# First attention: each iteration's value products split in two column groups, with the maxima's products between them

## The reference, cut to what matters

```python
# x: 2 batches x 1024 tokens x 128; 16 heads, 8 numbers a head for q and k, 64 for v
cp = leaky_relu(einsum('btd,cd->btc', representations, Wc) + bc)
q, k, v = ...                                    # (2, 1024, 16, 8), (2, 1024, 16, 8), (2, 1024, 16, 64)
scores = einsum('bqhd,bkhd->bhqk', q, k) / 8 ** 0.5
attn = softmax(scores, axis=-1)
out = einsum('bhqk,bkhd->bqhd', attn, v).reshape(2, 1024, 1024)
proj = leaky_relu(einsum('btv,dv->btd', out, Wo) + bo)
```

## Time and profile before

| | us |
|---|---|
| median of 3 runs | 991.14 (988.55 to 994.42) |
| the profiled execution's own time | 985.0 |
| its span | 983.2 |
| first attention in that span (from 152 to 608) | 456 |

### The profile page before, as it was taken

How to read it: one execution, slowest core, us unless ns; L and a number is a source line. 1 busy time by engine, 2 the same in 40 slices (tenths; PEclk the granted TensorE clock), 3 DMA queues, 4 the chain that set the end, 5 groups by cost and what they waited for, 6 DMA issues and landing times. The chain is left out here.

```text
span 983.2 us, 20738 instructions
## 1 busy us (share of the span) xinstructions
PE 894.0 (91%) x7627; PEld 471.3 (48%) x7627; DVE 766.7 (78%) x1324; ACT 537.4 (55%) x903; POOL 599.2 (61%) x533
## 2 busy tenths in 40 slices
PE   4899997999999999899998999789999778799996
PEld 2356562233333333233332233679887444478695
DVE  6997789888888888998888852894589999983413
ACT  2154455666766676566666676454365334375463
POOL 3670327668887776878698876106527787572323
PEclk9899998999999999999999999999999999999999
DMA  9362364011111201102111113548761001253562
GB/s 314 117 208 86 105 195 145 16 41 47 32 57 29 65 25 31 49 22 74 40 40 38 40 35 110 169 140 262 217 188 62 23 24 52 68 164 106 161 180 83
DMA packets 90339, 94.86 MB, mean 96 GB/s; under 512 B 23136, under 2 KB 67296, under 8 KB 89984
## 3 DMA queue, kind: packets, MB, share of 16 engines
q1 hardware_dynamic: 85120, 83.04, 27.5%
q0 software_dynamic: 5120, 10.50, 3.7%
HBM read 68.79 MB, written 24.25 MB: 95 GB/s over the span
## 5 line engine op out<-in xcount | busy, mean ns | idle before, releaser
L254 PE MATMUL ps<-ar 64*64 64x512 f32 (+3 forms) x5244 | 518.7, 446 | 28.1 <-DVE small L276 8.9
L254 PEld LDWEIGHTS ps<-ar 64*64 64x64 f32 (+2 forms) x5244 | 254.3, 135 | 275.7 <-ACT ar L300 84.1
L300 ACT ACTIVATE ar<-ps 128x1024 f32<-128x1024 f32 (+1 forms) x302 | 284.0, 944 | 117.5 <-PE ps L254 111.3
L276 DVE TENSOR_REDUCE small<-ps 128x2 f32<-128x1024 f32 (+2 forms) x276 | 306.6, 1139 | 46.6 <-PE ps L254 44.7
L263 POOL TENSOR_TENSOR psum_sb<-psum_sb,ar 128x1024 f32<-128x1024 f32 x91 | 214.8, 2360 | 53.1 <-DVE on_sb L263 41.9
L263 POOL TENSOR_TENSOR ar<-ar 128x512 f32<-128x512 f32 (+1 forms) x80 | 80.0, 1004 | 45.4 <-DVE ar L276 22.3
L322 POOL DMA_INDIRECT gT<-ysort,rt x48 | 48.0, 999 | 92.8 <-issue 91.5
L263 DVE TENSOR_TENSOR ar<-ps,ar 128x256 f32<-128x256 f32 (+4 forms) x48 | 50.5, 1059 | 55.2 <-PE ps L254 51.4
L263 POOL TENSOR_TENSOR psum_sb<-ar 128x1024 f32<-128x1024 f32 x32 | 75.8, 2370 | 23.8 <-ACT ar L300 16.6
L297 ACT COPY ar<-ps 128x256 f32<-128x256 f32 (+2 forms) x84 | 30.8, 378 | 72.7 <-PE ps L254 33.3
L254 PE MATMUL ps<-wA,xnT 128*128 128x512 f32 (+3 forms) x208 | 60.8, 419 | 4.0 <-DVE rt L268 1.8
(11 more groups left out here) (160 smaller groups left out, 1077.2 us busy)
## 6 DMA issues: line engine op xcount, KB each, us to landing
ar<-in_L_up SPq DMA_DIRECT2D x46, 384.0 KB, 4.0
ar<-in_L_b SPq DMA_DIRECT2D x30, 322.0 KB, 3.6
rec_sb<-lscr SPq DMA_DIRECT2D x64, 128.0 KB, 2.9
scr<-ar SPq DMA_DIRECT2D x48, 128.0 KB, 2.6
ar<-xsort SPq DMA_DIRECT2D x36, 128.0 KB, 3.9
ysort<-ar SPq DMA_DIRECT2D x36, 128.0 KB, 1.9
ar<-scr SPq DMA_DIRECT2D x32, 112.0 KB
ar<-scr SPq DMA_DIRECT2D x32, 96.0 KB
```

What stands on the lines that cost most here:

```text
L254: return self.e.matmul(o, l, r, start=start, stop=stop) if self.e else Nothing()
L276: return self.e.tensor_reduce(o, a, AX.X, op, negate=True) if negate else self.e.tensor_reduce(o, a, AX.X, op)
L300: return self.e.activation(o, a, fn, **kw) if self.e else Nothing()
```

## The change

For `kt` 1 to 7 the value products of an iteration become two groups, queries 0 to 255 and 256 to 511 of each of the four matmuls. The first group stands ahead of the maxima's products and the second behind them. For `kt == 0` the four matmuls keep their 512 columns (the flag that starts a sum afresh works on a whole bank) and stand, whole, ahead of the maxima's products. The semaphore that says that `pv` is done sits on the second group.

```diff
-        def pv(i):
+        def pv(i, z):
             g, pr, hf, kt = SCHED[i]
             tile = 8 * (g // 4) + kt
-            if kt == 0:
-                pe.wait_ge(*vacant(6))
-                pe.wait_ge(*vacant(7))
-            pe.wait_ge(*at("exp", i))
+            if z and kt == 0:
+                return
+            x0, w = 256 * z, 256 if kt else 512
+            if z == 0:
+                if kt == 0:
+                    pe.wait_ge(*vacant(6))
+                    pe.wait_ge(*vacant(7))
+                pe.wait_ge(*at("exp", i))
             for n in range(2):
                 r = slice(64 * n, 64 * n + 64)
                 for a in range(2):
                     h = 4 * (g % 4) + 2 * pr + a
-                    ins = pe.mm(ps[64 * a:64 * a + 64, 6 + n, :],
+                    ins = pe.mm(ps[64 * a:64 * a + 64, 6 + n, x0:x0 + w],
                                 V0[r, 1024 * tile + 64 * h:1024 * tile + 64 * h + 64],
-                                Ps[r, i % NP, 512 * a:512 * a + 512], start=kt == 0, stop=kt == 7)
-                if kt == 7:
+                                Ps[r, i % NP, 512 * a + x0:512 * a + x0 + w], start=kt == 0, stop=z > 0 and kt == 7)
+                if z and kt == 7:
                     ins.then_inc(*filled(6 + n, ("pvd" if n else "pvd_low", i)))
-            if kt < 7:
+            if (z and kt < 7) or kt == 0:
                 ins.then_inc(*up(("pvd", i)))
...
                 pairs = searched(i)
+                if i >= LAG:
+                    pv(i - LAG, 0)
                 for p in pairs[:1]:
                     max_pair(*p, (take(ring[0]),))
                 if i >= LAG:
-                    pv(i - LAG)
+                    pv(i - LAG, 1)
                 tails(i)
...
-            pv(254)
-            pv(255)
+            for z in range(2):
+                pv(254, z)
+            for z in range(2):
+                pv(255, z)
```

## The result

The changed kernel takes 1006.26 us (median of four runs, 1005.87 to 1006.84) against 989.85 for the kernel before (985.72 to 994.42). The ratio is 1.0178, with a 95% interval from 1.0142 to 1.0213: slower, as forecast, by 16.4 us where the sum had 11.0. The profiled execution took 1006.84 with a span of 1005.0 (before: 985.0 and 983.2).

The account below looks back on a forecast made before the run. PE was taken as nearly full (437.0 of 456.0 us), DVE close behind (379.0). Terms over 32 units summed to +11.0, turning the profiled 985.0 into 996.0 and, by the runs' median, 1002 us; range 996 to 1009.

Parts of the forecast that it names:

- PE lives on its distance to DVE: Within an attention unit, PE depends on DVE's distance to the banks it must free; plain unit +0.42 us.
- D2: Start of DVE's maximum in iteration 2, the first behind the sums, counted from that iteration's scores: 0.68 becomes 1.54.
- S4: Start of iteration 4's scores, which wait for the maximum two iterations earlier: 2.61 becomes 2.82, +0.21 us.
- The passes at 0.22: Value products in seven of eight iterations: four 256-column passes take 0.87 against 0.86, +0.01 us an iteration.
- The gain of 0.27: Maxima's products no longer wait for the previous scores' exponential: 0.17 once and 0.03 three times, together -0.27 us a unit.
- 5 with transposes: Units with the small transposes, where scores wait for an exponential and maxima's products for a maximum: +0.41 each, +2.0 us.
- 3 with the long scaling: Units whose scaling takes 1.28 beside a POOL addition: -0.2 if clear, +0.4 if not, +0.1 taken; +0.3 us in all.
- 2 with gating: Units where a 1.36 gating operation on DVE holds a maximum and scores wait: +0.86 each, +1.7 us in all.
- 8 mixed: Units where PE waits for later stages' routing and normalisation: bounds 0 and +0.9, +0.3 taken each, +2.4 us.
- Faster: Rival: DVE catches up by its idle 1.37, so the scores' wait does not appear; -6 us, 985; chance 14%.
- No change: Rival: plain units lose, but mixed and early units gain 0.27 and long scalings vanish; +3.8 at most, 993; chance 12%.
- Dearer passes: Rival: each of the four shorter value passes costs 0.02 more than its columns; +15 us on top, 1017; chance 6%.

Follow-up runs that it names:

- the second pair: One more profile each of the unmodified kernel before and the changed kernel, on the chips of the experiments: 988.84 and 1004.77 us.
- the first experiment: Changed kernel with its short passes kept, but all value products put back behind the maxima's products; ratio 1.0024 to the kernel before.

## Why the prediction was right, point by point

*PE lives on its distance to DVE* held, to a hundredth. In the plain unit the prediction had D2 at 1.54, the scaling at 2.68, D3 at 3.28, D6 at 7.12; the rows give 550.34, 551.48, 552.08 and 555.92, less 548.80: 1.54, 2.68, 3.28, 7.12. S4 was to come at 2.82 and S5 at 4.55; they do. The unit was to take 13.88 and takes 13.86, since the passes behind the waits keep 1.295 from scores to scores.

*The passes at 0.22* held: six groups, four of them passes, fill an iteration of 1.295, and the kernel with the passes alone loses 0.02 a unit.

*The gain of 0.27* held, and can be seen by itself: 13.46 - 13.19 in the kernel with the first product back behind, the 0.02 of the passes included.

*By classes of units*, measured as differences between the first two profiles:

| units | predicted | measured |
|---|---|---|
| 8 plain | +3.4 | +3.6 |
| 5 with transposes | +2.0 | +1.5 for four, +3.5 for the fifth |
| 3 with the long scaling | +0.3 | -0.1 |
| 2 with gating | +1.7 | +1.7 |
| 8 mixed | +2.4 | +3.0 |
| 2 early | +1.0 | +0.7 |
| last ones | +0.2 | +0.8 |
| behind and ahead of the attention | 0 | +7.1 |

The sum of 11.0 was for the attention, which grew by 14.8 (13.8 in the second pair). Of the 3.8 between them 3.1 is the fifth unit with transposes, 0.6 the mixed units and 0.6 the last ones; the rest comes to -0.6. Six of the eight plain units took the +0.40 worked out for them, two took +0.56 and +0.59, for a reason that was not traced. The mixed units lie between -0.20 and +1.53, so that a guess of +0.3 each came near their sum by luck.

Transposes: 14.34 where 14.37 was worked out, though by a step I had missed. The transposes wait themselves, for D3, 0.70 (the first row); it costs nothing, as the maxima's products behind them wait until D4 all the same (the second row, S2 at 347.31):

```profile
351.86 0.10 PEld L257 LDWEIGHTS ps<-cb,small 64*48 64x48 bf16 x2 [0.70 <-DVE small L276]
...
352.99 2.98 PEld L254 LDWEIGHTS ps<-ar 64*64 64x64 bf16 x60 [0.72 <-DVE small L276]
```

Gating: 15.07 where 15.10 was worked out, by luck in one term (the length of the gating operation, see below). The last ones: one of the units that I had counted as being without maxima still has them, and it alone cost 0.86. That was a wrong count, not a wrong mechanism.

*The long scaling and the fifth unit with transposes* are one term, and it was mis-sized. I had two answers for the scaling beside POOL's addition, and took the middle. What decides is one rule that the rows of before already held. DVE's scaling and POOL's first addition of the unit, in one unit of the kernel before:

```profile
399.96 2.60 DVE L263 TENSOR_TENSOR on_sb<-osb,rec_sb 128x512 f32<-128x512 f32 x1
```

```profile
399.66 2.36 POOL L263 TENSOR_TENSOR psum_sb<-ar 128x1024 f32<-128x1024 f32 x1
```

and in the unit of the changed kernel that lost most:

```profile
500.16 2.51 DVE L263 TENSOR_TENSOR on_sb<-osb,rec_sb 128x512 f32<-128x512 f32 x1
```

```profile
499.77 2.35 POOL L263 TENSOR_TENSOR psum_sb<-ar 128x1024 f32<-128x1024 f32 x1
```

402.56 is 0.54 behind the end of POOL's 402.02, and 502.67 is 0.55 behind 502.12. In the earlier trace rows it is 233.17 behind 232.62, 0.55 too. Over the 41 such pairs in six traces (both kernels twice, and the two versions with the first product back and with the scaling later) the scaling ends 0.54 to 0.56 behind the addition whenever it starts while the addition runs, and takes 0.68 to 0.73 when it starts clear of it. So it isn't slowed: it stands still until POOL's instruction is done. The Trainium skill says so, "SBUF — State Buffer", section "SBUF: two separate sides": the port pair of the two engines is an exclusive lock held for a whole instruction, against a DVE operation with two SBUF inputs and a GpSimd operation that reads SBUF; the trace agrees, with the 0.54 to 0.56 above.

The gating operation, which reads `acc_sb` and `gT`, goes by the same rule, and the prediction took its 1.36 for its own length. In all ten traces those gating operations of the attention that start beside one of POOL's additions (27 between 300 and 380 us) end 0.14 to 0.16 behind it. In the kernel with the scaling later they meet none under way and take 0.30 to 0.34:

```profile
338.59 0.30 DVE L271 SCALAR_TENSOR_TENSOR gT<-acc_sb,rt,gT 128x128 f32<-128x128 f32 x1
```

There the two gating units take 13.92, less than the 14.24 of the kernel before. In the changed kernel the addition had moved along with the operation, which kept 1.33: that is the luck in the 15.07. With the first product back it took 1.15, which is the 0.22 by which those units came out shorter than expected.

By that rule the three units with the long scaling are plain to work out. The addition has moved too (233.40 against 230.26), the scaling waits only for its last 0.32 and takes 0.87, and the unit has 14.52, between my two answers. In the fifth unit the scaling of before started clear, 0.68; moved 0.86 later within its unit, it meets an addition that has just begun. It ends 1.83 later than alone, D3 with it, and the transposes' load waits 2.53:

```profile
503.86 0.10 PEld L257 LDWEIGHTS ps<-cb,small 64*48 64x48 bf16 x2 [2.53 <-DVE small L276]
```

Behind that hole the granted clock is 0.50, the 1.2 GHz level, for 3.40 us (the window from 504.90), in which PE is busy 3.31: up to half of that, 1.65, is time lost to the clock, by this estimate. The other four units of the class come to 14.34 in the changed kernel; 1.83 and 1.62 more make the 17.79 of this one, so the clock takes nearly all of that bound. (Measured against the kernel before it is 3.47 too, since there this unit took 14.32: its sums waited 1.06 for POOL, a wait that is gone.) The second profile of the changed kernel shows both again (2.53 for the scaling, the half clock from 505.1); in the version with the scaling an iteration later, the same unit takes 15.04 in place of 17.79, with a scaling of 1.38.

*Mixed units.* Half of their +3.0 is one unit, +1.5, in which PE waits for routing and the clock then falls:

```profile
539.22 6.94 PE L254 MATMUL ps<-ar 64*64 64x512 bf16 x96 [2.62 <-DVE rt L268]
```

The kernel before has that hole as well, 2.63 at 527.31, and no fall behind it; the changed kernel has the fall in both profiles. What makes the difference is not settled. The place alone does not decide in general: in the two profiles of the kernel before, the same hole of 2.13 us, at 403.95 and 404.34, has no fall behind it in the first and this one in the second, where the unit takes 18.97 in place of 17.38:

```profile
404.30:407.70 3.40, 3.36 (x20) 0.86 (x24) 2.35 (x2) 1.02 (x1) 3.26 (x2) 0.50 0.00 0
```

*Outside of the attention* "unchanged in length" failed in the first pair of profiles: 7.1 of the 21.8 by which their spans differ lie there. 0.8 of it is ahead. Behind, 374.00 and 380.20 us of windows hold the same program; for the kernel before its row is:

```profile
608.20:982.20 374.00, 325.53 (x2208) 256.99 (x2200) 262.64 (x572) 172.41 (x429) 179.74 (x202) 0.98 0.42 126
```

The same work keeps PE busy 334.23 in place of 325.53, at a granted clock of 0.95 in place of 0.98; DVE, ACT and POOL are as before. So this part goes with the clock. It begins at the first normalisation behind the attention:

```profile
631.13 1.28 PE L254 MATMUL ps<-wA,ar 128*128 128x128 f32 x4 [2.08 <-DVE ar L279]
```

PE's hole of 2.08 stood there before, too, with 1.63 and no fall behind it; now the half clock lasts from 631.2 to 638.0, and in the second profile of the changed kernel from 631.4, behind a hole of 1.96. Most of the 7.1 does not come back. In the second pair, of two chips, the spans differ by 16.0 and the attentions by 13.8, which leaves 2.2; the medians differ by 16.4, which leaves 1.6 to 2.6. The first profile of the kernel before, 985.0, is shorter than every other run of that kernel (985.56 to 994.42). Behind the attention the kernel before has 375.0 in one profile and 377.8 in the other, with 18.9 and 21.5 us at half clock; the changed one has 381.3 and 379.2, with 41.3 and 35.6. Nor does the stretch go by the order of the products: with short maxima the kernel before has 381.0 and the changed one 377.7. The version with the first product back, whose attention is the shortest of those with full maxima, has 381.5, and so loses in its profile what its attention gains; its whole runs come out 1.8 shorter. What the change itself does to this part, if anything, stays open; no run here tells it from chance.

*The rivals.* Faster needed D2 to end before 2.56; it ended at 2.77, so the price was paid in every plain unit. With the first product put back it is what happens, in the attention. No change needed the mixed and the early units to gain and the long scalings to vanish; they came to +3.0, +0.7 and -0.1. Dearer passes fell with the first experiment.

## What to carry to other kernels

When two engines hand buffers round a ring, read from the trace by how much each hand-over clears, then shift the one you move and carry the lateness along the slower engine's queue until a gap takes it up: that gave the times of plain units and of units with transposes to 0.03 us. Moving work ahead of a product is free only where the reader of that product has slack; here it has none in the first iteration after its idle stretch, and leaving that one iteration alone turns the change from +14.8 us in the attention to -4.1. Check also which operations of two engines hold each other up when they come to overlap: here the cost isn't a share, it is the whole rest of the other's instruction, and a long operation in a trace may be a short one that waits.

## What the runs showed of the hardware

- DVE's operation with two inputs in SBUF (128x512, 0.68 alone) stands still while POOL adds two tiles of 128x1024 (2.36), and ends 0.54 to 0.56 behind it: 0.76 to 2.80 us, by where it starts. The gating operation (128x128, 0.30 to 0.34 alone) does the same and ends 0.14 to 0.16 behind. Maxima, which read PSUM, take 1.17 to 1.23 beside the same additions, as they do elsewhere.
- A hole of PE of 1.96 to 2.62 us is followed, at some places, by 3.4 or 6.8 us at the 1.2 GHz level. In the changed kernel three such places repeat in both profiles; in the kernel before, a hole of 2.63 us has no fall behind it in either, and one of 2.13 us in one of the two.
- A float32 pass of 256 columns in four quarters of 64x64 takes 379 ns, one on the whole array 380, and two of them take PE no longer than one of 512 columns: 28 passes in place of 14 cost a unit 0.02 us.
